# Attention scores from packed stationary tiles, with Q's products moved two sub-steps ahead

## The chip, the cores and the metric

The kernel runs on one core of a Trainium2 chip. The metric is the time of one execution on the device in microseconds (us). Three runs of the kernel before took 1155.66, 1157.41 and 1158.08 us, median 1157.41. The engines are TensorE (PE in the profile; its weight loads stand apart as PEld), VectorE (DVE), ScalarE (ACT), GpSimd (POOL) and SyncE (SP), which issues nearly all DMAs.

## The reference

Cross-attention of x (32 elements of 512 rows by 512) on a short context (32 by 77 by 512), 16 heads of depth 32, with a residual and a layer norm. In short:

```python
qh = _split_heads(q @ wq.T + bq, h)          # q: (32, 512, 512)
kh = _split_heads(k @ wk.T + bk, h)          # k = v = context: (32, 77, 512)
vh = _split_heads(v @ wv.T + bv, h)
scores = einsum('ntd,nsd->nts', qh, kh) / sqrt(32)
scores = scores + repeat(mask, h, axis=0)[:, None, :] * PAD
attn = softmax(scores, axis=-1)
ctx = einsum('nts,nsd->ntd', attn, vh)
out = _merge_heads(ctx, h) + q
out = (out - mean(out)) / sqrt(var(out) + 1e-5) * gamma + beta
```

## The kernel before

**Precision by parts.** Products are taken in fp32r, which keeps fewer bits than float32. So an operand is held as a high part (rounded) and a low part (what the rounding left), and a product is high times low plus low times high plus high times high: three matmuls (`terms`). This holds for Q, K, V and for the scores.

**Phase one** (0 to about 131 us) projects the context to K and V for all elements and stores both in scratch memory. K is masked, its mean over the kept keys is taken off (DVE sums, POOL makes `k_shift` from `shift_of_key` and adds it, ACT and DVE write the high and low parts). At its end two of the four column groups of the first element's Q are made.

**Phase two** runs a pipeline of steps over the elements; a loop does most of them, two a round. A step has 8 sub-steps, s = 0 to 7; h = s // 4 is one half of the heads (8 heads, two groups g of four), t = s % 4 is a tile of 128 rows of x. In each sub-step TensorE does, in this order:

- `q_half`: half of the product of one column group g of Q, 6 matmuls of 512 columns (two sub-steps make a group);
- `scores` of element a, half h, tile t: for each of two groups, three matmuls of 308 columns (four heads times 77 keys) with a 128-row piece of Q as weights; K stands as a block diagonal, `bd`, 32 rows of it to a head;
- `turn`: transposes of the exponents of the half before, a tile of up to 128 (head, key) pairs at a time, four transposes to a tile, five tiles to a half, by the table TURNS = ([], [0, 1], [2, 3], [4]) over t;
- `product`: attention times V for element a - 1, ten matmul instructions.

Beside it, ACT rounds Q from PSUM to `q_hi` with its bias (`high_q`), takes the exponent, copies turned tiles from `t_ps` to `pt` (`copy_pt`), rounds x (`high_x`) and normalises rows (`norm`). DVE makes `q_lo` (`q_low`), row maxima, the subtraction of the maximum, the scaling by the sum (`inv_sum`, `attn`), and the statistics. POOL makes the low part of x (`split_x`), adds x, and applies gamma and beta.

The order on each engine is that of its `step` function; nothing else schedules. PSUM has eight banks: two scores tiles of two banks each, two `t_ps`, one `q_ps`, one `o_ps`. A turn waits until the tile two before it has been copied out of its bank. The low and high parts of Q are for a group done in the sub-step after its second half, and the scores of the next half use them at once.

## Time and profile before

| | |
|---|---|
| median of three runs | 1157.41 us |
| the profiled execution | 1157.28 us, its span 1155.5 us |
| TensorE busy | 1123.1 us (97%) |
| weight loads | 1037.8 us (90%) |
| DVE, ACT, POOL busy | 822.1 (71%), 612.5 (53%), 771.8 us (67%) |
| mean granted TensorE clock | 0.988 of full |
| DMA | 141.07 MB, queue of SP 40.1% of 16 engines |

Busy time is what an engine's instructions cover. A matmul's time runs from its start to when its last result is written, and the next starts well before that; the pace of a stream of matmuls is therefore read from the starts of successive rows, or from the chain of waits, whose pieces follow one another without overlap.

### The profile page before, as it was taken

The page shows a single profiled execution, that of the slowest core. Times are in us where ns is not written, and L with a number is a line of the kernel's source. Part 1 is how long each engine was busy: PE and PEld are TensorE (multiplying, and loading weights), DVE is VectorE, ACT ScalarE, POOL GpSimd, SP SyncE. Part 2 cuts the span into 40 slices and gives each one's busy share as a digit, 9 for nine tenths or more (in the row PEclk, how much of TensorE's full clock was granted, in tenths as well). Part 3 has the DMA queues.
Part 4 walks back from the last instruction along what each step waited for, and adds up shares of the span by engine and source line. Part 5 has one row for each costly group of instructions (what it writes and reads, how often), then busy time and mean ns, then how long its engine had stood idle before and what let it go on. Part 6 is the DMA issues. An engine that isn't in the chain of part 4 may idle for free.

```text
span 1155.5 us, 25702 instructions
## 1 busy us (share of the span) xinstructions
PE 1123.1 (97%) x7541; PEld 1037.8 (90%) x7541; DVE 822.1 (71%) x1622; ACT 612.5 (53%) x1008; POOL 771.8 (67%) x667
## 2 busy tenths in 40 slices
PE   7899999999999999999999999999999999999994
PEld 7788789999999999999999999999999999999983
DVE  5776467777777777777777777777777777777786
ACT  3321254556566555555555656655555555565551
POOL 4999523677766676766667776667676666777465
PEclk9999999999999999999999999999999999999996
DMA  7745433233343444343344333344443334333223
GB/s 228 261 147 188 150 104 90 74 122 95 116 119 117 126 126 126 116 120 99 102 123 122 106 105 119 117 126 126 126 116 122 98 102 123 123 101 110 85 82 128
DMA packets 147207, 141.07 MB, mean 122 GB/s; under 512 B 86452, under 2 KB 88004, under 8 KB 147172
## 3 DMA queue, kind: packets, MB, share of 16 engines
q1 hardware_dynamic: 146564, 140.29, 40.1%
q10 hardware_dynamic: 608, 0.33, 0.1%
q8 instruction: 20, 0.33, 0.1%
q14 instruction: 15, 0.12, 0.0%
HBM read 91.71 MB, written 48.85 MB: 122 GB/s over the span
## 4 chain that ended last, share of the span: by engine, by line
PE 84%; DVE 2%; POOL 1%; issue 0%; ACT 0%; DMA 0%; DVEq 0%; SPq 0%; POOLq 0%
PE q_ps L724 31%; PE o_ps L765 23%; PE s_ps L740 18%; PE t_ps L751 12%; POOL x_lo L991 0%; DVE stats L822 0%; DVE attn L853 0%; PE q_ps L765 0%; DVE y L862 0%; DMA xT_raw<-in_xT 0%; DVE attn L814 0%; DVE row_max L885 0%; DVE y L868 0%; ACT q_hi L1030 0%; DVE y L843 0%
## 5 line engine op out<-in xcount | busy, mean ns | idle before, releaser
L765 PE MATMUL o_ps<-v_tiles,pt 128*128 128x66 f32 x2520 | 310.7, 270 | 1.5 <-DVE attn L814 1.5
L765 PEld LDWEIGHTS o_ps<-v_tiles,pt 128*128 128x128 f32 x2520 | 304.0, 192 | 1.9 <-issue 1.9
L885 DVE TENSOR_REDUCE row_max<-s_ps 128x8 f32<-128x616 f32 x256 | 203.2, 794 | 118.2 <-PE s_ps L740 118.1
L740 PE MATMUL s_ps<-bd,q_hi 128*128 128x308 f32 x1024 | 260.5, 305 | 1.1 <-ACT q_hi L1030 1.1
L991 POOL TENSOR_TENSOR x_lo<-xT_raw,x_hi 128x512 fp32r<-128x512 f32 x124 | 159.3, 1286 | 117.8 <-ACT x_hi L1026 117.7
L961 POOL TENSOR_TENSOR attn<-attn,x_rows 128x512 f32<-128x512 f32 x124 | 160.2, 1292 | 115.8 <-DVE attn L814 115.8
L1036 ACT COPY pt<-t_ps 128x512 f32<-128x512 f32 (+1 forms) x320 | 175.0, 588 | 107.1 <-PE t_ps L751 107.0
L1030 ACT ACTIVATE q_hi<-q_ps,bq_col 128x512 fp32r<-128x512 f32 x125 | 86.1, 689 | 254.9 <-PE q_ps L724 254.9
L724 PE MATMUL q_ps<-x_lo,wq_hi 128*128 128x512 f32 x500 | 218.7, 437 | 2.5 <-PEq L142 2.1
L1016 ACT ACTIVATE probs<-probs 128x616 f32<-128x616 f32 x256 | 183.3, 716 | 64.3 <-DVE probs L894 64.3
L894 DVE TENSOR_TENSOR probs<-s_ps,row_max 128x616 f32<-128x616 f32 x256 | 204.6, 799 | 5.7
L724 PE MATMUL q_ps<-x_hi,wq_lo 128*128 128x512 f32 x500 | 197.6, 395 | 0.0
L724 PE MATMUL q_ps<-x_hi,wq_hi 128*128 128x512 f32 x500 | 197.4, 395 | 0.0
L740 PEld LDWEIGHTS s_ps<-bd,q_hi 128*128 128x128 f32 x1024 | 181.1, 189 | 12.9 <-ACT q_hi L1030 1.5
L875 DVE SCALAR_TENSOR_TENSOR q_lo<-q_ps,bq_col,q_hi 128x512 fp32r<-128x512 f32 x125 | 93.8, 751 | 114.2 <-ACT q_hi L1030 114.2
L751 PE MATMUL t_ps<-ident,probs 128*128 128x128 f32 (+1 forms) x1280 | 171.9, 273 | 0.0
L969 POOL TENSOR_TENSOR y<-attn,gamma_all 128x512 f32<-128x512 f32 x123 | 158.5, 1288 | 13.8 <-ACT attn L1040 13.8
L972 POOL TENSOR_TENSOR y<-y,beta_all 128x512 f32<-128x512 f32 x123 | 158.5, 1289 | 9.6
L740 PE MATMUL s_ps<-bd,q_lo 128*128 128x308 f32 x512 | 156.3, 305 | 0.0
L751 PEld LDWEIGHTS t_ps<-ident,probs 128*128 128x128 f32 (+1 forms) x1280 | 151.1, 139 | 1.1
L814 DVE TENSOR_TENSOR attn<-o_ps,inv_sum 128x256 f32<-128x256 f32 x252 | 106.9, 424 | 17.9
L724 PEld LDWEIGHTS q_ps<-x_hi,wq_hi 128*128 128x128 f32 x500 | 94.1, 188 | 22.6
(96 smaller groups left out, 1292.9 us busy)
## 6 DMA issues: line engine op xcount, KB each, us to landing
xT_raw<-in_xT SPq DMA_DIRECT2D x128, 256.0 KB, 3.5
x_rows<-in_x SPq DMA_DIRECT2D x32, 1024.0 KB, 5.6
out<-y SPq DMA_DIRECT2D x128, 256.0 KB, 2.1
k_scratch<-k_out SPq DMA_DIRECT2D x8, 1232.0 KB, 5.4
bd<-k_scratch SPq DMA_DIRECT2D x128, 77.0 KB, 2.4
v_scratch<-v_out SPq DMA_DIRECT2D x16, 264.0 KB
v_tiles<-v_scratch SPq DMA_DIRECT2D x256, 9.9 KB
ctx_raw<-in_ctxT SPq DMA_DIRECT2D x3, 1232.0 KB, 6.2
```

What stands on the lines that cost most here:

```text
L724: mm = pe.matmul(q_bank(b, g)[:, :], (wq_hi, wq_lo)[u][:, k, P * g:P * g + P], x_part[v][:, k, :], start=(k == 0 and n == 0), stop=(k == K ...
L740: mm = pe.matmul(s_ps[t % 2][:, j, 0:GS], (q_hi, q_lo)[u][:, g, P * t:P * t + P], bd[par][:, v, g, :, :].rearrange("p h s -> p (h s)"), st ...
L751: mm = pe.transpose(t_ps[(NT * h + i) % 2][0:w, P * t:P * t + P], probs[h][:, t, P * i:P * i + w], ident[:, :])
L765: mm = pe.matmul(bank_of(b, t)[:, col:col + tile_cols[i]], pt[h][0:w, i, P * t:P * t + P], v_tiles[v_buffer(b, h)][0:w, i, 0:tile_cols[i]] ...
L885: dve.tensor_reduce(row_max[:, u, :].rearrange("p (j h) -> p j h", j=2), score_heads(t), AX.X, ALU.max).then_inc(max_ready, 1)
L894: dve.tensor_tensor(probs[h][:, t, :].rearrange("p (j h s) -> p j h s", j=2, s=S), score_heads(t), row_max[:, u, :].rearrange("p (j h) -> ...
L961: pool.tensor_tensor(attn[par][:, t, :], attn[par][:, t, :], x_rows[:, t, :], ALU.add).then_inc(resid_done, 1)
L969: pool.tensor_tensor(y[par][:, t, :], attn[par][:, t, :], gamma_all[:], ALU.mult).then_inc(scaled, 1)
L972: pool.tensor_tensor(y[par][:, t, :], y[par][:, t, :], beta_all[:], ALU.add).then_inc(out_ready, 1)
L991: pool.tensor_tensor(x_lo[par][:, k, :], xT_raw[:, k, :], x_hi[par][:, k, :], ALU.subtract).then_inc(x_lo_ready, 1)
L1016: act.activation(probs[h][:, t, :], probs[h][:, t, :], ACT.Exp).then_inc(exp_done, 1)
L1036: act.copy(pt[h][0:w, i, :], t_ps[(NT * h + i) % 2][0:w, :]).then_inc(pt_ready, 1)
```

## The change

**Packed weights for the scores.** The three products of a group of four heads used the array's 128 rows as four heads of 32 each. Now three tiles hold the parts of Q in another arrangement. `q_a`: rows 0 to 95 the high parts of heads 0 to 2, rows 96 to 127 a copy of head 0's high part. `q_c`: rows 0 to 95 the low parts of heads 0 to 2, rows 96 to 127 head 1's high part. `q_b`: head 3's high part, head 3's low part, head 2's high part, head 3's high part. K's tiles `k_ac` and `k_b` hold K's high or low parts to match. The matmuls with `q_a` and `q_c` write three heads (3 times 78 = 234 columns), the one with `q_b` writes heads 2 and 3 (156 columns). The 12 products of head parts are the same as before. A head takes 78 columns in place of 77 (`SW`).

**What it asks of the others.** A group's high part takes two ACT instructions (`q_a`, 96 partitions; `q_b`, 64), its low part two on DVE (96 and 32). Three DMAs for each pair of groups, issued by ACT (`move_q`), copy 32-row pieces within the on-chip memory; `scores` waits for them (`q_moved`). K of an element comes by 12 DMAs of 32 rows, before by 4 with twice the data each; they stand after x's in SP's order.

**Order of the work.** `q_of_step` puts Q's products two sub-steps earlier. Q has two PSUM banks (`q_ps`), turned tiles one (`t_ps`); a turn now waits for the copy of the tile just before it. The turns are spread as the tables TURNS_AHEAD and TURNS_BEHIND say (ahead of or behind the scores of the sub-step). `high_x` is at s = 2, 3, 4, 6, `norm` at s = 4, 6, 7 and at s = 0 of the next step; the store of row tile 1 and some of POOL's scaling move too. ACT does `copy_pt` before it issues `move_q`.

**Phase one.** POOL no longer makes `shift_of_key`: DVE multiplies each sum by the negative reciprocal count (`minus_mean_of_keys`). The zeroing of K's tiles comes after the first chunk, the mask's transposes after the first V tile. gamma and beta are loaded at the start of phase two, and DVE and POOL wait for them there (`scale_loaded`).

TensorE in the third sub-step (t = 2) of a step before: the rest of Q's half product, the scores of the element (`s_ps`), two turns (`t_ps`), the first products with V.

```order
L724 MATMUL q_ps<-x_hi,wq_hi 128x512
L740 MATMUL s_ps<-bd,q_hi 128x308 [waits k_loaded_0,shifted,q_lo_ready,q_hi_ready]
L740 MATMUL s_ps<-bd,q_lo 128x308
L740 MATMUL s_ps<-bd,q_hi 128x308 x2
L740 MATMUL s_ps<-bd,q_lo 128x308
L740 MATMUL s_ps<-bd,q_hi 128x308
L751 MATMUL t_ps<-ident,probs 128x128 [waits pt_ready,exp_done]
L751 MATMUL t_ps<-ident,probs 128x128 x3
L751 MATMUL t_ps<-ident,probs 128x128 [waits pt_ready,exp_done]
L751 MATMUL t_ps<-ident,probs 128x128 x3
L765 MATMUL o_ps<-v_tiles,pt 128x66 [waits attn_ready,v_loaded_0,pt_ready]
```

The same engine and sub-step now:

```order
L811 MATMUL q_ps<-x_hi,wq_hi 128x512
L842 MATMUL t_ps<-ident,probs 128x128 [waits pt_ready,exp_done]
L842 MATMUL t_ps<-ident,probs 128x128 x3
L828 MATMUL s_ps<-k_ac,q_a 128x234 [waits k_loaded_1,q_moved_0,shifted,q_lo_ready,q_hi_ready]
L828 MATMUL s_ps<-k_ac,q_c 128x234
L831 MATMUL s_ps<-k_b,q_b 128x156
L828 MATMUL s_ps<-k_ac,q_a 128x234
L828 MATMUL s_ps<-k_ac,q_c 128x234
L831 MATMUL s_ps<-k_b,q_b 128x156
L842 MATMUL t_ps<-ident,probs 128x128 [waits pt_ready,exp_done]
L842 MATMUL t_ps<-ident,probs 128x128 x3
L856 MATMUL o_ps<-v_tiles,pt 128x66 [waits attn_ready,v_loaded_0,pt_ready]
```

One turn has moved ahead of the scores; between the two turns, which share a bank, stand six narrower matmuls.

ACT in two sub-steps before, from the rounding of a group of Q on (`q_hi`; `pt` are copies of turned tiles, `probs` exponents):

```order
L1030 ACTIVATE q_hi<-q_ps,bq_col 128x512 [waits q_done]
L1016 ACTIVATE probs<-probs 128x616 [waits shifted]
L1036 COPY pt<-t_ps 128x512 [waits turned] x2
L1016 ACTIVATE probs<-probs 128x616 [waits shifted]
L1036 COPY pt<-t_ps 128x512 [waits turned] x2
```

ACT now, from the second sub-step to the third:

```order
L1136 ACTIVATE q_a<-q_ps,bq_col 96x512 [waits q_done]
L1138 ACTIVATE q_b<-q_ps,bq_col 64x512
L1153 COPY pt<-t_ps 128x512 [waits turned]
L1145 DMA q_a<-q_a 32x1024 [waits q_hi_ready]
L1146 DMA q_c<-q_a 32x1024
L1148 DMA q_b<-q_b 32x1024
L1116 ACTIVATE probs<-probs 128x616 [waits shifted]
L1153 COPY pt<-t_ps 128x512 [waits turned]
L1126 CAST x_hi<-xT_raw 128x512 [waits scores_done,xT_loaded_0]
L1153 COPY pt<-t_ps 128x512 [waits turned]
```

A group's rounding is two instructions, three DMA issues follow, and between the two copies of the third sub-step stands the rounding of x.

The diff, cut to its core:

```diff
-    GS = HG * S
+    GS = HG * (S + 1)
...
-    KDMA = HG * DMA
+    KDMA = 3 * HG * DMA
+    QDMA = 3 * DMA
...
-    KS = 6
+    KS = 5
+    SW = S + 1
+    QW = 3 * DH
...
+        q_a = sb(whole, "q_a", [P, NG, T], F32R)
+        q_b = sb(whole, "q_b", [P, NG, T], F32R)
+        q_c = sb(whole, "q_c", [P, NG, T], F32R)
+        k_ac0 = sb(whole, "k_ac0", [P, 2, NG, 3, SW], F32R)
+        k_b0 = sb(whole, "k_b0", [P, NG, 2, SW], F32R)
...
-                pool.tensor_tensor(shift_of_key[:], keep[:], neg_rcount[:].unsqueeze(3).broadcast_to([P, NG, 2, S]),
-                                   ALU.mult).then_inc(keep_set, 1)
-                pool.memset(bd0[:].bitcast(F32), 0.0).then_inc(bd_zeroed, 1)
...
-                        pool.tensor_tensor(k_shift[:], shift_of_key[:, m, :, :].unsqueeze(1).broadcast_to([P, HB // 2, 2, S]),
+                        pool.tensor_tensor(k_shift[:], keep[:, m, :, :].unsqueeze(1).broadcast_to([P, HB // 2, 2, S]),
...
+                    if c == 0:
+                        pool.memset(k_ac0[:].bitcast(F32), 0.0).then_inc(bd_zeroed, 1)
+                        pool.memset(k_b0[:].bitcast(F32), 0.0).then_inc(bd_zeroed, 1)
...
+                act.wait_ge(q_hi_ready, 4)
+                act.dma_start(q_a[QW:P, 0:2, :].bitcast(F32), q_a[0:DH, 0:2, :].bitcast(F32)).then_inc(q_moved[0], DMA)
+                act.dma_start(q_c[QW:P, 0:2, :].bitcast(F32), q_a[DH:2 * DH, 0:2, :].bitcast(F32)).then_inc(q_moved[0], DMA)
+                act.dma_start(q_b[0:DH, 0:2, :].bitcast(F32), q_b[QW:P, 0:2, :].bitcast(F32)).then_inc(q_moved[0], DMA)
...
+                    dve.wait_ge(k_totalled, n + 1)
+                    dve.tensor_tensor(k_sum[:, slot, :, :], k_sum[:, slot, :, :],
+                                      neg_rcount[:, n % NG, :].unsqueeze(1).broadcast_to([P, HB // 2, 2]), ALU.mult
                                       ).then_inc(k_summed, 1)
...
-            t_ps = [ps(two, f"t_ps{i}", [P, BANK]) for i in range(2)]
-            q_ps = ps(two, "q_ps", [P, BANK])
+            t_ps = ps(two, "t_ps", [P, BANK])
+            q_ps = [ps(two, f"q_ps{i}", [P, BANK]) for i in range(2)]
...
+            X_STEPS = (2, 3, 4, 6)
...
-            TURNS = ([], [0, 1], [2, 3], [4])
+            TURNS_AHEAD = ([], [], [2], [])
+            TURNS_BEHIND = ([0], [1], [3], [4])
...
             def q_bank(b, g):
-                return o_ps if isinstance(b, int) and b == 0 and g % 2 == 1 else q_ps
+                return q_ps[g % 2]
+            def q_of_step(s):
+                half, u = (s + 2) // 4, (s + 2) % 4
+                return (half + 1) // 2, (0 if half == 1 else 2) + u // 2, u % 2
...
+                    for ac in range(2):
+                        for h in range(3):
+                            rows = slice(DH * h, DH * h + DH)
+                            sp.dma_start(k_ac[par][rows, ac, :, h, 0:S].bitcast(F32), k_dram[b, rows, 0, :, :]
+                                         ).then_inc(k_loaded[par], DMA)
+                        rows = slice(DH * ac, DH * ac + DH)
+                        sp.dma_start(k_ac[par][QW:P, ac, :, ac, 0:S].bitcast(F32), k_dram[b, rows, 1, :, :]
                                      ).then_inc(k_loaded[par], DMA)
+                    for q in range(2):
+                        sp.dma_start(k_b[par][DH * q:DH * q + DH, :, 1, 0:S].bitcast(F32), k_dram[b, QW:P, 0, :, :]
+                                     ).then_inc(k_loaded[par], DMA)
+                        rows = slice(DH * (q + 2), DH * (q + 2) + DH)
+                        sp.dma_start(k_b[par][rows, :, q, 0:S].bitcast(F32), k_dram[b, rows, 1, :, :]
+                                     ).then_inc(k_loaded[par], DMA)
+                sp.dma_start(gamma_all[:], gamma.partition_broadcast(P)).then_inc(scale_loaded, DMA)
+                sp.dma_start(beta_all[:], beta.partition_broadcast(P)).then_inc(scale_loaded, DMA)
...
-                        used = b * 4 + g
-                        if isinstance(used, int) and used <= 4:
-                            used -= 1
-                        at_least(pe, q_hi_ready, used)
-                        at_least(pe, q_lo_ready, used)
+                        at_least(pe, q_hi_ready, b * 8 + (2 * g - 2))
+                        at_least(pe, q_lo_ready, b * 8 + (2 * g - 2))
...
-                    pe.wait_ge(q_hi_ready, b * 4 + (2 * h + 2))
-                    pe.wait_ge(q_lo_ready, b * 4 + (2 * h + 2))
+                    pe.wait_ge(q_hi_ready, b * 8 + (4 * h + 4))
+                    pe.wait_ge(q_lo_ready, b * 8 + (4 * h + 4))
+                    pe.wait_ge(q_moved[h], (b + 1) * QDMA)
                     pe.wait_ge(k_loaded[par], b * (KDMA // 2) + (KDMA - par * (KDMA // 2)))
                     at_least(pe, shifted, b * 8 + (4 * h + t - 1))
                     for j in range(2):
                         g = 2 * h + j
-                        for n, (u, v) in enumerate(terms):
-                            mm = pe.matmul(s_ps[t % 2][:, j, 0:GS], (q_hi, q_lo)[u][:, g, P * t:P * t + P],
-                                           bd[par][:, v, g, :, :].rearrange("p h s -> p (h s)"),
-                                           start=(n == 0), stop=(n == 2))
+                        for ac, q in ((0, q_a), (1, q_c)):
+                            pe.matmul(s_ps[t % 2][:, j, 0:3 * SW], q[:, g, P * t:P * t + P],
+                                      k_ac[par][:, ac, g, :, :].rearrange("p h s -> p (h s)"),
+                                      start=(ac == 0), stop=False, skip_group_check=True)
+                        mm = pe.matmul(s_ps[t % 2][:, j, 2 * SW:GS], q_b[:, g, P * t:P * t + P],
+                                       k_b[par][:, g, :, :].rearrange("p h s -> p (h s)"),
+                                       start=False, stop=True, skip_group_check=True)
                     mm.then_inc(scores_done, 1)
                 def turn(b, h, i):
                     pe.wait_ge(exp_done, b * 8 + (4 * h + 4))
-                    at_least(pe, pt_ready, b * (2 * NT) + (NT * h + i - 1))
+                    at_least(pe, pt_ready, b * (2 * NT) + (NT * h + i))
...
                         h, t = s // 4, s % 4
-                        qb = a + h
-                        g = (2 if h == 0 else 0) + t // 2
-                        if real(qb) and not in_phase_one(qb, g):
-                            q_half(qb, g, t % 2, (par + h) % 2)
+                        ahead, g, part = q_of_step(s)
+                        if real(a + ahead) and not in_phase_one(a + ahead, g):
+                            q_half(a + ahead, g, part, (par + ahead) % 2)
...
+                        if real(a - 1 + h):
+                            for i in TURNS_AHEAD[t]:
+                                turn(a - 1 + h, 1 - h, i)
                         if real(a):
                             scores(a, h, t, par)
...
                         if real(a - 1 + h):
-                            for i in TURNS[t]:
+                            for i in TURNS_BEHIND[t]:
                                 turn(a - 1 + h, 1 - h, i)
...
-                    dve.wait_ge(q_hi_ready, b * 4 + (g + 1))
-                    dve.scalar_tensor_tensor(out=q_lo[:, g, :], in0=q_bank(b, g)[:, :], scalar=bq_col[:, g:g + 1],
-                                             in1=q_hi[:, g, :], op0=ALU.add, op1=ALU.subtract
+                    dve.wait_ge(q_hi_ready, b * 8 + (2 * g + 2))
+                    dve.scalar_tensor_tensor(out=q_c[0:QW, g, :], in0=q_bank(b, g)[0:QW, :], scalar=bq_col[0:QW, g:g + 1],
+                                             in1=q_a[0:QW, g, :], op0=ALU.add, op1=ALU.subtract
                                              ).then_inc(q_lo_ready, 1)
+                    dve.scalar_tensor_tensor(out=q_b[DH:2 * DH, g, :], in0=q_bank(b, g)[QW:P, :],
+                                             scalar=bq_col[QW:P, g:g + 1], in1=q_b[QW:P, g, :],
+                                             op0=ALU.add, op1=ALU.subtract).then_inc(q_lo_ready, 1)
...
+                dve.wait_ge(scale_loaded, 2 * DMA)
...
+                pool.wait_ge(scale_loaded, 2 * DMA)
...
+                    if g == 0:
+                        at_least(act, scores_done, b * 8 - 4)
+                    if g == 2:
+                        at_least(act, scores_done, b * 8)
+                    act.activation(q_a[0:QW, g, :], q_bank(b, g)[0:QW, :], ACT.Identity, bias=bq_col[0:QW, g:g + 1]
                                    ).then_inc(q_hi_ready, 1)
+                    act.activation(q_b[P // 2:P, g, :], q_bank(b, g)[P // 2:P, :], ACT.Identity,
+                                   bias=bq_col[P // 2:P, g:g + 1]).then_inc(q_hi_ready, 1)
+                def move_q(b, h):
+                    act.wait_ge(q_hi_ready, b * 8 + (4 * h + 4))
+                    g = slice(2 * h, 2 * h + 2)
+                    act.dma_start(q_a[QW:P, g, :].bitcast(F32), q_a[0:DH, g, :].bitcast(F32)).then_inc(q_moved[h], DMA)
+                    act.dma_start(q_c[QW:P, g, :].bitcast(F32), q_a[DH:2 * DH, g, :].bitcast(F32)
+                                  ).then_inc(q_moved[h], DMA)
+                    act.dma_start(q_b[0:DH, g, :].bitcast(F32), q_b[QW:P, g, :].bitcast(F32)).then_inc(q_moved[h], DMA)
...
                         if real(a - 1 + h):
-                            for i in TURNS[t]:
+                            for i in TURNS_AHEAD[t]:
                                 copy_pt(a - 1 + h, 1 - h, i)
+                        for k in range(KC):
+                            if X_STEPS[k] == s and real(a + 2):
+                                high_x(a + 2, k, par)
+                        ahead, g, part = q_of_step(s)
+                        high = part == 1 and real(a + ahead) and not in_phase_one(a + ahead, g)
+                        if high:
+                            high_q(a + ahead, g)
+                        if real(a - 1 + h):
+                            for i in TURNS_BEHIND[t]:
+                                copy_pt(a - 1 + h, 1 - h, i)
+                        if high and g % 2 == 1:
+                            move_q(a + ahead, g // 2)
```

## Rows read from the trace of the kernel before

**Rows 1.** The page, part 1: busy us (share of span) xinstructions.

```profile
PE 1123.1 (97%) x7541; PEld 1037.8 (90%) x7541; DVE 822.1 (71%) x1622; ACT 612.5 (53%) x1008; POOL 771.8 (67%) x667
```

**Rows 2.** The chain of waits that ended last, 690 to 725 us: start, us, what.

```profile
691.72 1.45 PE q_ps L724 x6
693.17 0.85 PE s_ps L740 x6
...
694.89 1.06 PE o_ps L765 x10
...
722.98 1.45 PE q_ps L724 x6
```

**Rows 3.** Timeline, TensorE, 693 to 696 us: start, us, engine, line, op, tiles, count.

```profile
693.15 0.30 PE L740 MATMUL s_ps<-bd,q_lo 128*128 128x308 f32 x1
...
693.85 1.04 PE L751 MATMUL t_ps<-ident,probs 128*128 128x128 f32 x8
694.73 1.23 PE L765 MATMUL o_ps<-v_tiles,pt 128*128 128x66 f32 x10
```

**Rows 4.** The same stretch, weight loads.

```profile
693.15 0.33 PEld L740 LDWEIGHTS s_ps<-bd,q_hi 128*128 128x128 f32 x2
...
694.62 1.20 PEld L765 LDWEIGHTS o_ps<-v_tiles,pt 128*128 128x128 f32 x10
```

**Rows 5.** Groups by line and shape: busy us, mean ns | idle before.

```profile
L740 PE MATMUL s_ps<-bd,q_hi 128*128 128x308 f32 x1024 | 260.5, 305 | 1.1 <-ACT q_hi L1030 1.1
...
L765 PE MATMUL o_ps<-v_tiles,pt 128*128 128x99 f32 x1008 | 209.3, 289 | 0.0
...
L1036 ACT COPY pt<-t_ps 128x512 f32<-128x512 f32 x256 | 137.5, 589 | 104.5 <-PE t_ps L751 104.5
...
L875 DVE SCALAR_TENSOR_TENSOR q_lo<-q_ps,bq_col,q_hi 128x512 fp32r<-128x512 f32 x125 | 93.8, 751 | 114.2 <-ACT q_hi L1030 114.2
...
L1030 ACT ACTIVATE q_hi<-q_ps,bq_col 128x512 fp32r<-128x512 f32 x125 | 86.1, 689 | 254.9 <-PE q_ps L724 254.9
...
L1036 ACT COPY pt<-t_ps 104x512 f32<-104x512 f32 x64 | 37.5, 585 | 2.6 <-PE t_ps L751 2.5
```

**Rows 6.** Stretch of two elements: us, then busy us of PE, PEld, DVE, ACT, POOL.

```profile
691.50:754.10 62.60, 62.60 (x435) 58.23 (x434) 45.31 (x93) 36.45 (x60) 42.93 (x37) 1.00 0.38 116
```

**Rows 7.** Timeline, 713 to 715 us, a turn and its copies.

```profile
713.72 1.04 PE L751 MATMUL t_ps<-ident,probs 128*128 128x128 f32 x8
...
714.35 1.07 ACT L1036 COPY pt<-t_ps 128x512 f32<-128x512 f32 x2 [1.34 <-PE t_ps L751]
```

**Rows 8.** Timeline, 1111 to 1113 us, a wait of TensorE.

```profile
1111.65 0.42 DVE L814 TENSOR_TENSOR attn<-o_ps,inv_sum 128x256 f32<-128x256 f32 x1
...
1112.22 1.30 PE L765 MATMUL o_ps<-v_tiles,pt 128*128 128x66 f32 x10 [0.50 <-DVE attn L814]
```

**Rows 9.** Timeline, 37 us, a wait of TensorE in phase one.

```profile
37.51 0.48 PE L522 MATMUL v_ps<-wv_lo,ctx_hi 128*104 128x512 f32 x1 [2.98 <-DVE v_out L420]
```

**Rows 10.** Stretch behind it: us, busy us by engine; after them the granted clock.

```profile
37.50:41.00 3.50, 3.49 (x10) 2.46 (x11) 2.04 (x4) 1.26 (x3) 3.06 (x5) 0.61 0.92 310
```

**Rows 11.** Timeline: DMA issues by ACT (4 us), phase two's start.

```profile
3.99 0.89 ACTq L339 DMA_DIRECT2D keep<-in_mask  x2
...
132.33 0.47 PE L724 MATMUL q_ps<-x_lo,wq_hi 128*128 128x512 f32 x1 [2.09 <-PEq L142]
...
135.67 5.04 POOL L991 TENSOR_TENSOR x_lo<-xT_raw,x_hi 128x512 fp32r<-128x512 f32 x4
```

**Rows 12.** Timeline of SP's DMA issues, 690 and 720 us.

```profile
690.47 2.89 SPq L670 DMA_DIRECT2D bd<-k_scratch  x4
...
720.65 0.38 SPq L661 DMA_DIRECT2D out<-y  x1
```

**Rows 13.** DMA issues: count, KB each, median us to landing.

```profile
bd<-k_scratch SPq DMA_DIRECT2D x128, 77.0 KB, 2.4
...
gamma_all<-in_gamma SPq DMA_DIRECT2D x1, 256.0 KB, 5.4
```

More of the change, by code:

```diff
@@ L96, in xattn @@
         q_lo_ready = sem("q_lo_ready")
+        q_moved = [sem(f"q_moved_{i}") for i in range(2)]
         x_hi_ready = sem("x_hi_ready")
@@ L688, in step @@
                                      ).then_inc(x_loaded, DMA)
+                    if real(a + 1) and not in_phase_one(a + 1):
+                        load_keys(a + 1, 1 - par)
                     if real(a - 3):
+                        store(a - 3, 1, 1 - par)
                         store(a - 3, 2, 1 - par)
@@ L1035, in copy_pt @@
                     w = tile_rows[i]
-                    act.copy(pt[h][0:w, i, :], t_ps[(NT * h + i) % 2][0:w, :]).then_inc(pt_ready, 1)
+                    act.copy(pt[h][0:w, i, :], t_ps[0:w, :]).then_inc(pt_ready, 1)
                 def norm(b, t, par):
```

197 lines of the change are left out of this document (119 added, 78 removed).

## The prediction

> **What bounds the kernel now.** I read the page first: TensorE is busy 97% of the span, its weight loads 90%, no other engine over 71% [rows 1]. Then the chain of waits inside the loop: in 690 to 725 us it holds TensorE pieces alone, six matmuls for Q (1.45 us), six for the scores (0.85), ten for V (1.06), with turns between, and the same place of the next element comes 722.98 - 691.72 = 31.26 us later [rows 2]. Two elements take 62.60 us and TensorE is busy in all of them, at full clock (1.00); DVE is busy for 45.31 of them, ACT for 36.45, POOL for 42.93 [rows 6]. So in the loop every nanosecond that TensorE's stream loses or gains is the kernel's, until another engine comes late.
>
> Last, the paces. A score matmul of 308 columns takes 0.85 / 6 = 0.141 us [rows 2]. Its row says 305 ns, since a row runs to the last result, about 0.16 us past the next one's start. A transpose of 128 columns takes (694.73 - 693.85) / 8 = 0.109 us [rows 3]. V's weight loads: 1.20 us for ten, one alone 0.33 - 0.14 = 0.19, so (1.20 - 0.19) / 9 = 0.112 us each [rows 4]. These matmuls have 66 and 99 columns, the transposes 128, and all come at 0.11: it is the weight load that paces them, and the columns do not show.
>
> **Term A, the narrower scores.** Still three matmuls for a group, 1536 in all in 512 groups, but of 234, 234 and 156 columns in place of 308 each. None of them should be paced by its columns: 308 cost 0.141, 512 cost 1.45 / 6 = 0.242, that is 0.0005 us a column, which puts 234 at 0.104 and 156 at 0.066. Both lie below the load's 0.112. So a group costs 3 x 0.112 = 0.336 in place of 0.423, and 512 groups save 512 x 0.087 = **44.5 us**. Bounds: if the load did not pace them, 0.274 a group and -76 us; above, no gain at all (0.141 stays the price), or a loss (the third rival). The trace has no fp32r matmul under 308 columns. I take the load's pace, since it holds for 66, 99 and 128 columns.
>
> The row pair at 693.15 shows a weight load starting with the matmul before it, which is still running, at the same rows of the array [rows 3, 4]. The Trainium skill, TensorE: Matmul & The Clock Gate, section "Packing small matmuls — row/col tiling", says that a load overlaps matmuls in flight only when it goes to another row group. By that a group would cost its loads and its columns one after the other, about 0.34 + 0.27 = 0.61, and the change would lose 96 us; but 308 columns and a load at 0.141 together already contradict it.
>
> The same page, section "Back-to-back issue gap", gives a sustained 81 ns a matmul at 128 columns and 131 at 512. By it (an estimate) a group costs 0.27, and A is -78 us. The rows disagree at both ends: 109 ns at 128 columns, 242 at 512 [rows 2, 3].
>
> **Term B, a new wait between two turns.** With one `t_ps` bank a turn waits for the copy of the one before. Four of the five have a product or Q's matmuls between them. Turns 2 and 3 have only the scores. From turn 2's start: its four transposes take 4 x 0.109 = 0.44, the last result is there at 0.61 (the eight of [rows 7] last 1.04 = 8 x 0.109 + 0.17), the copy starts 0.03 later (714.35 against 714.32 by the same sum) and takes 0.589 [rows 5, 7], so it ends at 1.23. From a release to TensorE's next matmul it takes 1112.22 - 1112.07 = 0.15, and a stream that restarts is 0.07 longer (1.30 against 1.23 for the same ten) [rows 3, 8]: 1.45. Without the wait turn 3 would start at 0.44 + 6 x 0.112 = 1.11. The loss is 0.34, two times an element: 64 x 0.34 = **+21.8 us**. It is not less if ACT is busy when the tile comes, only more. At that point ACT has behind it the exponent and the three DMA issues, about 0.47 each (0.89 for two [rows 11]); they end about 1.2 us into the sub-step and turn 2 ends at 1.45 + 0.61. So ACT is free, with some 0.2 us to spare behind the exponent. Behind the waiting turn on TensorE stand its product and the next Q half; all slip with it. Bounds: 0 (if I am wrong on the copy) and 0.6 each, 38 us.
>
> **Term C, more work for DVE and ACT.** A group's low part is now two instructions; partitions do not shorten one (ACT's copy takes 589 ns on 128 and 585 on 104 partitions [rows 5]). DVE: 8 more in two elements at 751 ns, less 0.08 of overlap, 5.4 us: 45.31 + 5.4 = 50.7 of about 61 us, 83% [rows 5, 6]. ACT: 8 more roundings at 689 ns less 0.10 of overlap, 4.7, and 12 DMA issues at 0.47, 5.6: 46.7 of 61. Both hold on average. They are close in the odd sub-steps, the more so as DVE's statistics fall in two of them (s = 1, 7); the product then waits for `attn`, since `o_ps` is one bank. I take **+1.5 us**, bounds 0 and +25. The Q parts themselves have two sub-steps, about 7.5 us, where they had none. The on-chip copies of 128 KB each should land in 2.4 us, as K's 77 KB did [rows 13], or in twice that, and are covered. Gone with `q_ps` as a single bank is a wait that the loop did not have: nothing.
>
> **SP.** K's load goes from 4 issues in 2.89 us [rows 12] to 12 of half the size, some 6 us. The queue is 9 us idle between V's pieces and the store at 720.65 [rows 12]. What it is moved past, x's loads and the residual's, starts 2.9 us sooner; K has until the next step. Nothing.
>
> **Term D, phase one.** TensorE waits 2.98 us for `v_out` at 37 us [rows 9], and the 3.50 us behind it ran at clock 0.61 [rows 10], which is 1.4 us lost at 1.2 GHz. The wait ends a chain that starts with POOL's `shift_of_key` and the zeroing, both gone from there. I take **-4 us**, bounds 0 and -4.4.
>
> **Term E, the start of phase two.** ACT and DVE each have two instructions more, and ACT three DMA issues, between the last Q product and the barrier: +1.2. Then DVE and POOL wait for gamma and beta, 5.4 us from issue to landing [rows 13], the second 0.4 later; POOL's four `x_lo` take 5.04 [rows 11]. They would end about 10.7 us after the barrier. TensorE now wants them after four Q halves and two scores, 4 x 1.45 + 2 x 0.67 = 7.1. That is a wait of about 3.5, where 1.06 stood (for Q's high part [rows 5]). With another half-clock stretch of 1.5 possible I take **+4.5 us**, bounds 0 and +8.
>
> **The sum**, against the profiled execution's own 1157.3 us (the median is 1157.4, so it stands for the runs): 1157.3 - 44.5 + 21.8 + 1.5 - 4 + 4.5 = **1136.6 us**. An element takes 31.26 - 1.39 + 0.68 + 0.05 = 30.6 us.
>
> **Rivals.**
> 1. The turn's wait does not show (the copies come in time): for it, before a turn had 0.87 us of other work around it and no wait; against it, the sum of B, made of rows. Time 1136.6 - 21.8 = 1114.8. Chance 0.17.
> 2. DVE is the bound where both statistics and low parts fall. For it: in sub-step 7 its instructions sum to about 4.1 us against 3.6 of TensorE's. Against it: sub-steps 2 to 4 give it back. If each element loses 0.6 us more, 32 x 0.6 = 19 us: 1155.8. Chance 0.11.
> 3. The other side: a narrow fp32r matmul runs at the price of a plain float32 one. The place is the scores of every sub-step. The nearest row is V's 99 columns, float32, 289 - 162 = 127 ns, 1.28 ns a column [rows 5]. A group of 624 columns is then 0.80, +0.377 x 512 = +193, and the turn's wait is covered: 1157.3 + 193 + 1.5 + 0.5 = 1352 us. It decides from the point at which a group costs over 0.423 less the rest of the sum, about 0.38. Against it: the cost of 308 and of 512 columns falls with the columns. For it: only that no row lies under 308. Chance 0.12.
> 4. The change doesn't do what it says: narrow matmuls keep 0.141. Then A is 0, and with 0.85 between the turns B is 64 x 0.16 = 10.4: 1157.3 + 10.4 + 1.5 - 4 + 4.5 = 1169.7. Chance 0.05.
>
> **How the numbers follow.** My forecast has 0.55; by its own bounds it lies between 1122 and 1150. The predicted time is 1136.6. The range runs from 1108, below rival 1 by the bounds of D and E, to 1158, which takes in rival 2; it leaves out rivals 3 and 4. A difference of 0.2% (2.3 us) is about what a measurement of this kernel can tell from none. Faster: 0.55 + 0.17 + 0.07 of rival 2 = 0.79; same: the rest of rival 2, 0.04; slower: rivals 3 and 4, 0.17.
>
> **What would show it.** A: six score matmuls in about 0.67 us between the first score and what follows. B: waits of TensorE for ACT's `pt`, 64 of them, some 0.34 us each, in the third sub-step of each half, and none at the other turns. C: DVE near 83% with no wait of TensorE for it. D: no wait for `v_out` at 37 us and no half clock behind it. E: one wait for `x_lo` of some 3 us early in phase two. I am wrong if the six take more than 0.8 us, if DVE's `attn` or ACT's exponent shows up as what TensorE waits for in the loop, or if the turns wait over 0.6 us.

## The result and the profile after

The changed kernel takes 1148.68 us (median of six runs, 1145.06 to 1151.02), the kernel before, run beside it, 1155.0: a ratio of 0.994, 95% interval 0.992 to 0.996. Measured again later it was 1147.84 against 1155.88, ratio 0.9925 (0.990 to 0.995). So it is 6 to 8 us faster, where 21 were forecast. The profiled execution took 1145.06, span 1143.3.

The page after, part 1, answers to [rows 1] (busy us, share of the span, instructions), and part 4, the chain that ended last, by engine:

```profile
PE 1095.9 (96%) x7541; PEld 989.2 (87%) x7541; DVE 941.6 (82%) x1782; ACT 726.6 (64%) x1136; POOL 770.0 (67%) x668
...
PE 56%; DVE 14%; issue 8%; ACT 7%; ACTq 3%; DVEq 0%
```

TensorE is still busy nearly all the time, but it holds only 56% of the chain. The chain after, 690 to 725 us, a part of what stood as TensorE alone in [rows 2] (start, us, what):

```profile
698.94 1.45 PE q_ps L811 x6
700.39 0.22 PE s_ps L828 x2
...
712.81 0.80 DVE row_max L981
...
714.36 0.74 DVE q_c L968
715.13 0.76 DVE q_b L971
715.92 0.22 DVE inv_sum L895
...
719.70 0.67 ACT q_a L1136
...
721.10 0.53 ACT pt L1153
721.65 0.61 ACTq L1146
722.29 0.63 ACTq L1148
...
723.67 0.56 ACT pt L1153
724.28 0.66 PE t_ps L842 x4
```

The pieces between TensorE's work are DVE's low parts, ACT's rounding of Q and its DMA issues. That is the list of suspects, not yet the causes. The waits of TensorE in 500 to 900 us, 13 elements (engine and line, what it waited for, us in total, times, longest):

```profile
PEld t_ps L842 <- ACT pt L1153: 6.0, 26, 0.4
PEld t_ps L842 <- issue: 3.2, 13, 0.3
PEld o_ps L856 <- issue: 1.3, 6, 0.2
PEld o_ps L856 <- DVE attn L907: 1.1, 7, 0.2
PE t_ps L842 <- ACT pt L1153: 0.7, 3, 0.3
```

There are three kinds, at four places of an element: turn 3 behind the copy of turn 2 (twice), turn 0 of sub-step 0 behind the exponent (once; the view says "issue" there, but the matmul starts 0.13 us after ACT's exponent ends, in nearly every element), and the product of sub-step 4 behind `attn` (once).

One number carries all that follows: the time of one element in the loop, taken from the start of the 25th score cluster (a sub-step's six matmuls) to that of the 249th, 28 elements. Before: (1096.42 - 220.21) / 28 = 31.29 us. After: (1083.91 - 224.26) / 28 = 30.70. The forecast was 0.66 less an element; it is 0.59 less. The loop nearly kept its promise, but by errors that cancelled, as the runs show. What else is missing lies at the start of phase two and at the end.

### The profile page after: what moved, and what is told of

Read it like the earlier page. It is cut to its first block, busy times and chain, and to the rows that moved or that the text cites. A ratio compares the mean times of both kernels' runs of the same rounds, so it can differ in the third digit from the quotient of the medians.

```text
span 1143.3 us, 26963 instructions
## 1 busy us (share of the span) xinstructions
PE 1095.9 (96%) x7541; PEld 989.2 (87%) x7541; DVE 941.6 (82%) x1782; ACT 726.6 (64%) x1136; POOL 770.0 (67%) x668
## 3 DMA queue, kind: packets, MB, share of 16 engines
q1 hardware_dynamic: 167044, 145.36, 44.5%
## 4 chain that ended last, share of the span: by engine, by line
PE 56%; DVE 14%; issue 8%; ACT 7%; ACTq 3%; DVEq 0%
PE q_ps L811 21%; PE o_ps L856 16%; PE t_ps L842 9%; PE s_ps L828 7%; DVE row_max L981 4%; ACT pt L1153 3%; DVE probs L990 2%; PE s_ps L831 2%; DVE stats L915 2%; DVE q_b L971 2%; ACT q_a L1136 2%; ACTq L1148 2%; ACTq L1146 2%; DVE q_c L968 1%; ACT q_b L1138 1%
## 5 line engine op out<-in xcount | busy, mean ns | idle before, releaser
L856 PE MATMUL o_ps<-v_tiles,pt 128*128 128x66 f32 x2520 | 314.0, 272 | 1.0 <-DVE attn L907 0.8
L1153 ACT COPY pt<-t_ps 128x512 f32<-128x512 f32 (+1 forms) x320 | 186.9, 584 | 82.1 <-PE t_ps L842 76.6
L842 PE MATMUL t_ps<-ident,probs 128*128 128x128 f32 (+1 forms) x1280 | 200.4, 280 | 12.4 <-ACT pt L1153 5.0
L842 PEld LDWEIGHTS t_ps<-ident,probs 128*128 128x128 f32 (+1 forms) x1280 | 140.0, 140 | 35.5 <-ACT pt L1153 11.7
L828 PE MATMUL s_ps<-k_ac,q_a 128*128 128x234 f32 x512 | 155.2, 303 | 3.5 <-DVE q_c L968 3.5
L828 PE MATMUL s_ps<-k_ac,q_c 128*128 128x234 f32 x512 | 141.3, 276 | 0.0
L1136 ACT ACTIVATE q_a<-q_ps,bq_col 96x512 fp32r<-96x512 f32 x126 | 85.6, 680 | 81.7 <-PE s_ps L831 59.7
L831 PE MATMUL s_ps<-k_b,q_b 128*128 128x156 f32 x512 | 123.0, 240 | 0.0
L811 PEld LDWEIGHTS q_ps<-x_lo,wq_hi 128*128 128x128 f32 x504 | 96.2, 191 | 16.7 <-issue 5.1
```

The costliest lines, as they stand in the source:

```text
L811: mm = pe.matmul(q_bank(b, g)[:, :], (wq_hi, wq_lo)[u][:, k, P * g:P * g + P], x_part[v][:, k, :], start=(k == 0 and n == 0), stop=(k == K ...
L828: pe.matmul(s_ps[t % 2][:, j, 0:3 * SW], q[:, g, P * t:P * t + P], k_ac[par][:, ac, g, :, :].rearrange("p h s -> p (h s)"), start=(ac == 0 ...
L842: mm = pe.transpose(t_ps[0:w, P * t:P * t + P], probs[h][:, t, P * i:P * i + w], ident[:, :])
L856: mm = pe.matmul(bank_of(b, t)[:, col:col + tile_cols[i]], pt[h][0:w, i, P * t:P * t + P], v_tiles[v_buffer(b, h)][0:w, i, 0:tile_cols[i]] ...
L1153: act.copy(pt[h][0:w, i, :], t_ps[0:w, :]).then_inc(pt_ready, 1)
```

## Experiments

"After" is 1148 us in the differences below, "an element" the number just defined; every ratio is to the kernel before, with its 95% interval.

| run | median us | ratio | an element |
|---|---|---|---|
| narrow matmuls alone, in the kernel before | 1106.63 | 0.957 (0.955-0.959) | 29.67 |
| moves issued by SyncE | 1141.67 | 0.988 (0.986-0.990) | 30.65 |
| turn 3 behind the product | 1149.02 | 0.994 (0.993-0.996) | 30.79 |
| low parts later | 1138.78 | 0.986 (0.984-0.988) | 30.48 |
| after, again | 1147.84 | 0.9925 (0.990-0.995) | 30.69 |
| low parts later and turn 3 behind | 1120.62 | 0.970 (0.968-0.972) | 29.87 |
| that and scaling early | 1116.39 | 0.966 (0.964-0.968) | 29.67 |
| that and moves by SyncE | 1117.37 | 0.967 (0.965-0.968) | 29.67 |
| one low part | 1138.46 | 0.986 (0.984-0.988) | 30.43 |
| one rounding | 1141.65 | 0.989 (0.987-0.991) | 30.62 |
| one of each | 1128.42 | 0.977 (0.975-0.979) | 30.12 |

### Narrow matmuls alone

```diff
-  s_ps[..., 0:GS], q[...], bd[...]                    # 308 columns, three times
+  first, end = (0, 234) if n < 2 else (GS - 156, GS)  # 234, 234, 156
+  s_ps[..., first:end], q[...], bd[...][:, first:end]
```

> The kernel before with nothing changed but the columns of its three score matmuls: 0 to 234, 0 to 234 and 152 to 308 in place of 308 each. What is left out: two of the three products for a part of the columns, so the scores are not the reference's. It prices term A with no other part of the change. Theory (from the trace after, where six score matmuls take 0.63 us when nothing waits, against 0.85 before): 0.22 us less in 256 sub-steps, -56 us, ratio 0.951, with no wait of TensorE in the loop, since ACT and DVE have their old work. Rival 1 (the price in my prediction, every one at the weight load's 0.112): -44.5 us, 0.961. Rival 2 (the shorter stream runs into another engine here already): less than 35 us, with waits of TensorE in the loop.

Measured: -50.0 us. The chain, 690 to 700 us:

```profile
690.70 1.45 PE q_ps L724 x6
692.16 0.63 PE s_ps L741 x6
692.78 1.10 PE o_ps L766 x10
693.89 1.44 PE q_ps L724 x6
695.33 0.63 PE s_ps L741 x6
695.96 0.89 PE t_ps L752 x8
```

Six matmuls take 0.63 us where they took 0.85 [rows 2], no wait of TensorE stands in the loop, and the product and the turns behind take 0.02 to 0.04 more than before. An element takes 1.62 us less. This is term A; it was worth 50 in the median (52 by the element), not 44.5, and not the 56 of the bare 0.22 either.

Where the difference comes from is seen in single rows. The matmuls of one cluster in the kernel after, where nothing waits, and the weight loads of one in this run:

```profile
136.90 0.27 PE L828 MATMUL s_ps<-k_ac,q_a 128*128 128x234 f32 x1
137.00 0.28 PE L828 MATMUL s_ps<-k_ac,q_c 128*128 128x234 f32 x1
137.12 0.24 PE L831 MATMUL s_ps<-k_b,q_b 128*128 128x156 f32 x1
137.19 0.31 PE L828 MATMUL s_ps<-k_ac,q_a 128*128 128x234 f32 x1
137.34 0.27 PE L828 MATMUL s_ps<-k_ac,q_c 128*128 128x234 f32 x1
```

```profile
692.10 0.30 PEld L741 LDWEIGHTS s_ps<-bd,q_hi 128*128 128x128 f32 x2
692.33 0.19 PEld L741 LDWEIGHTS s_ps<-bd,q_lo 128*128 128x128 f32 x1
692.44 0.19 PEld L741 LDWEIGHTS s_ps<-bd,q_hi 128*128 128x128 f32 x1
692.55 0.75 PEld L766 LDWEIGHTS o_ps<-v_tiles,pt 128*128 128x128 f32 x6
```

Inside the cluster the loads come every 0.11 us, as the prediction took it. The matmul behind the one of 156 columns starts 0.07 to 0.08 us after it, but the next one then 0.15, so inside a cluster nothing is won by that: over the loop the first five gaps add up to 0.56 us, five times 0.112. Only the last gap, to the product or the turn, is 0.078 where the forecast had 0.112. That is 0.034 a cluster, less what the matmuls behind give back.

In the Trainium skill, TensorE: Matmul & The Clock Gate, section "Packing small matmuls — row/col tiling", one sentence says that loads overlap matmuls in flight only in another row group. This trace contradicts it: six loads and matmuls at the same rows took 0.63 us together. (The same section elsewhere lets a load for the array's background weight buffer go ahead; no run here tells which buffer a load went to.)

### Moves issued by SyncE, and turn 3 behind the product

```diff
 # ACT's step
-  if high and g % 2 == 1: move_q(a + ahead, g // 2)
 # SyncE's step, ahead of load_keys and ahead of the first store
+  move_q(a, 1) ... move_q(a + 1, 0)
```

> The kernel after with the three on-chip copies of Q's parts issued by SyncE (ahead of K's load and ahead of the first store) in place of ACT, in the loop; those of phase one stay on ACT. It takes 1.85 us of issue off ACT two times an element. Theory (what TensorE waits for at the end of these chains is one t_ps bank, ACT's crowded seventh sub-step and DVE's low parts, and the issues lie in a sub-step where ACT has room): the exponent behind them comes up to 0.6 us earlier, but the copy of turn 2 behind it only some 0.05, so -2 to -5 us of the time after, ratio to before 0.990 to 0.993. Rival (the chain of waits taken at its word, where ACT's DMA issues and the idle behind them hold some 5% of the span): -17 us or more, ratio 0.98.

-6 us in the median, but only 0.05 an element, which is 1.6. The two profiled executions differ by 1.4 us, so the traces do not show where the rest of the median is; it stays open, as far as it is not the scatter of the end (below). The chain's share for ACT's DMA issues was no measure of what they cost: the copy of turn 2 that stands behind them in sub-step 2 starts about 0.08 us after its tile is ready (0.28 in three elements of 28), and 0.04 with the moves on SyncE.

```diff
-TURNS_BEHIND = ([0], [1], [3], [4])
+TURNS_BEHIND = ([0], [1], [], [4])
+TURNS_LAST = ([], [], [3], [])      # behind product(a - 1, h, t)
```

> The kernel after with the fourth of five turns moved behind the product of its sub-step, on TensorE, and its copy ahead of the next exponent on ACT. Between the two turns that share a sub-step stands then the scores and a product. It prices term B. Theory: the wait of 0.24 us net and the slower restart of 0.055 behind it go, two times an element, 0.57 us x 32 = -18 us of the time after, ratio to before 0.979. Rival 1 (the wait only moves, to the turn that now has Q's half alone between it and the next, or to the exponent behind the moved copy on ACT): 0 to -6 us. Rival 2: ACT's copy, now ahead of the exponent, delays turn 0 of the next half: slower than after.

Nothing is gained and 0.09 an element lost: rival 1, in a form I had not named. The two places went different ways: sub-step 6 takes 0.19 less (3.75 us for 3.94), sub-step 2 takes 0.28 more (4.27 for 3.98). The timeline in sub-step 2, with turn 3 gone from between scores and product:

```profile
724.23 0.76 DVE L975 SCALAR_TENSOR_TENSOR q_b<-q_ps,bq_col,q_b 32x512 fp32r<-32x512 f32 x1
...
725.62 0.42 DVE L911 TENSOR_TENSOR attn<-o_ps,inv_sum 128x256 f32<-128x256 f32 x1
...
726.19 0.55 PE L857 MATMUL o_ps<-v_tiles,pt 128*128 128x66 f32 x3 [0.41 <-DVE attn L911]
```

The product, now due earlier, waits for `attn`, which stands on DVE behind the two low parts of the sub-step before. Turn 3's wait had covered that one.

### Low parts later, then with the turn, then with the scaling

```diff
 # DVE's step: q_low from the end of odd sub-steps to behind the next scale_attn
+  low = {2: (a, 3), 4: (a + 1, 0), 6: (a + 1, 1), 0: (a, 2)}.get(s)
+  if low ...: q_low(*low)
```

> The kernel after with DVE's two instructions for Q's low part moved from the end of their sub-step to behind the next one's inv_sum and attn. Nothing is added or taken away. It tests whether the second low-part instruction costs the product that waits for o_ps (sub-step 4: 0.23 us an element in the trace after). Theory: that wait goes, 0.23 x 32 = -7.4 us of the time after, ratio to before 0.987, and no other place gets worse by over 0.1 us an element. Rival (DVE is full over the stretch, so the order doesn't matter): 0, the wait comes back as a later row_max and a later exponent.

-9 us, an element 0.22 less: the wait of sub-step 4 is gone from the trace, as forecast.

> The kernel after, unchanged, on the chip of the next three runs: their base, and a second trace of it. Theory: the loop's element takes 30.67 us again and every sub-step the same to 0.02, and what differs between two executions lies before 165 us and behind 1090 us, where TensorE's clock steps. Rival: the loop itself varies by more than 0.1 us an element.

The second trace agrees with the first: 30.69, and on average no sub-step of the loop differs by over 0.02 us.

> The kernel after with two edits that were tried singly: Q's low part behind the next inv_sum and attn on DVE, and the fourth turn behind the product on TensorE (its copy on ACT now behind the next exponent). Theory (the first edit frees o_ps in time, which is what took back the second one's gain when it was alone): both waits go, 0.57 + 0.23 = 0.80 us an element, -25 us of the time after, ratio to before about 0.972. Rival (DVE is full around the statistics, so the product goes on waiting for attn): what the low parts alone gave, ratio 0.986.

-27 us, 0.83 an element. One edit alone gained 0.22, the other alone lost 0.09. Sub-step 2, where the moved turn alone had uncovered the wait for `attn`, now takes 3.65. One thing besides the pairing differs: ACT copies turn 3 behind the next exponent here and ahead of it in the run of the turn alone. That copy falls into sub-steps 3 and 7, which differ by 0.04 us at most between the two runs, so it hardly carries the result; no run separates it. The waits in 500 to 900 us shrink to one line, turn 0's:

```profile
PEld t_ps L843 <- issue: 2.6, 13, 0.2
```

```diff
 # ACT's step, s == 7
+  norm(a - 2, 2, par)      # now ahead of high_q, was behind copy_pt
   high_q(a + ahead, g)
```

> The run before it with one more edit: ACT's scaling of an attention row in the eighth sub-step stands ahead of Q's rounding, where ACT was idle for about 1 us, and no more between the copy and the next exponent. Theory: the exponent that turn 0 waits for comes 0.8 us earlier, and turn 0's wait of 0.32 us an element goes: -10 us of that kernel's time, -35 of the time after, ratio to before 0.963. Rival (the scaling waits for POOL's shift there and now holds Q's rounding, or DVE's probs comes last anyway): 0 to -3 us of that kernel's time.

0.20 an element, 4.2 us in the median (less than the 10 I gave it, since turn 0's wait and its restart had 0.25 in this kernel). TensorE has no wait left in the loop, and an element takes 29.67 us, exactly what it took with the narrow matmuls alone in the kernel before. So in this order the added instructions, the DMA issues, the single `t_ps` bank and K's smaller loads cost the loop nothing; all of the 1.03 us an element that the change lost against the narrow matmuls is taken back by order alone. The page's parts 1 and 4:

```profile
PE 1073.7 (97%) x7541; PEld 985.9 (89%) x7541; DVE 940.6 (85%) x1782; ACT 711.5 (64%) x1136; POOL 768.7 (69%) x668
...
PE 82%; DVE 2%; issue 1%; ACT 1%; DMA 1%; POOL 0%; SPq 0%; ACTq 0%; DVEq 0%; POOLq 0%
```

This kernel beats both: 0.966 of before, 0.973 of after, by order alone. Run again later it was 0.968 (0.966 to 0.970). DVE is busier (85%) than where it was the trouble (82%).

> The run before it with the copies of Q's parts issued by SyncE in the loop. Theory: in the loop they gate nothing now, 0 to -2 us; the start and the end gain what they gained when it was the only edit (1 to 5 us): -1 to -7 us of that kernel's time. Rival: with the other waits gone the issues on ACT are what is left, over -8 us.

0.00 an element and +1 us: the issues on ACT gate nothing.

### What the added instructions cost

```diff
-  q_c low ... .then_inc(q_lo_ready, 1); q_b low
+  q_c low ... .then_inc(q_lo_ready, 2)            # one low part
-  q_a high ... .then_inc(q_hi_ready, 1); q_b high
+  q_a high ... .then_inc(q_hi_ready, 2)           # one rounding
```

> The kernel after without DVE's second low-part instruction for every element but the first (left out: the low part of the fourth head's Q, which stays the first element's). It prices the added instruction by itself. Theory: the product's wait for attn in sub-step 4 (0.23 us an element) goes as it did when the instructions were only put later: -6 to -9 us of the time after, and DVE is busy for 91 us less. Rival 1: DVE's work as such costs (0.76 us x 4 an element): over -20 us. Rival 2: only the order mattered and one instruction is still in the way: 0.

> The kernel after without ACT's second rounding for every element but the first (left out: the fourth head's high part). Theory: the exponent that turn 0 waits for in sub-step 0 comes 0.7 us earlier and turn 0's 0.32 us go: -8 to -10 us of the time after; turn 3's wait stays. Rival: the exponent waits for DVE's probs anyway (DVE's low parts start earlier here, which helps): over -15 us or near 0.

> Both left out. ACT and DVE then have the counts of instructions for Q that they had before. It prices all of term C in the loop but for the DMA issues. Theory: the two waits are at two different places (sub-steps 4 and 0) and add up: -16 to -19 us of the time after; what is left to the kernel before with narrow scores alone is the one t_ps bank, 0.5 us an element. Rival: they overlap, -10 us.

In these three runs the fourth head's low part, its high part, or both are left out for every element but the first. One low part less: 0.27 an element, as expected. One rounding less: 0.08, a miss. Turn 0's wait in sub-step 0 went, but the product of the same sub-step now waits for `attn`: the sub-step takes 3.84 us, after 3.90, and 3.60 with both left out (waits, 500 to 900 us):

```profile
PEld t_ps L845 <- ACT pt L1157: 5.1, 26, 0.2
PEld o_ps L859 <- issue: 4.2, 20, 0.2
PEld o_ps L859 <- DVE attn L910: 1.2, 7, 0.2
```

Both: 0.58, far over the 0.35 of the parts, and only turn 3's wait is left:

```profile
PEld t_ps L845 <- ACT pt L1158: 5.3, 27, 0.2
```

So the added rounding and low part cost 0.58 an element, 18.7 us over 32, and the one `t_ps` bank 30.12 - 29.67 = 0.45, 14.4 us. This split of the 1.03 depends on the order of taking away, since the waits cover each other: with the low parts later, moving the turn was worth 30.48 - 29.87 = 0.61.

### The start of phase two

From the last matmul of phase one to the ninth score cluster it is 27.8 us before, 36.15 and 36.17 in the two traces after, 35.9 and 36.1 in those of the fastest kernel (scaling early). The chain after:

```profile
137.20 0.75 DVE q_c L968
137.98 0.76 DVE q_b L971
138.76 0.81 DVE row_max L981
139.60 0.81 DVE probs L990
140.43 0.72 ACT probs L1116
141.18 0.68 ACT q_a L1136
141.89 0.69 ACT q_b L1138
142.60 0.75 DVE q_c L968
143.38 0.76 DVE q_b L971
144.17 0.81 DVE row_max L981
```

Here DVE and ACT work in turn, each waiting for the other, with three groups' parts in series up to 149.3 us. The fifth cluster, at 149.41, also needs the moves: the last was issued at 143.81 and landed 5.4 us later, that is over the twice 2.4 us within which the prediction called them covered. The next runs change the fastest kernel for the first element alone (its second group pair); the first leaves the moves out, the second the added rounding and low part, the third both.

> The fastest kernel so far (low parts later, fourth turn behind the product, scaling early) without the copies of the second half of Q's parts of the first element alone; those partitions hold zeros for that element, so its scores for four heads are not the reference's. It prices the wait for these copies in the fifth sub-step of phase two, and what TensorE's clock does behind it. Theory: the fifth score cluster starts about 3 us earlier against the fourth, and the half-clock stretch behind it goes too: -4 us, 0.4% of that kernel's time. Rival 1: the next late thing there (x_lo, the exponent) takes its place: 0 to -1. Rival 2: the clock falls all the same: -3.

> The fastest kernel without ACT's second rounding and DVE's second low part for the second half of Q's groups of the first element alone (two groups; those rows hold zeros there, so four heads' scores of that element are not the reference's). It prices the chain at the start of phase two, which in the trace after runs from 135.7 to 149.4 us through ACT and DVE in turn, with three groups' parts in it. Theory: the chain loses 2 x (0.69 + 0.76) = 2.9 us, and the sixth score cluster comes 2.5 to 3 us earlier after the start of phase two: -2.5 to -4 us. Rival (the moves of Q's parts, which the fifth cluster waits for, hold it): the fifth cluster stays, less than -1.

> The same, and without the first element's copies of Q's second half either (which alone brought the fifth cluster 2.9 us forward and left the sixth where it was). Theory: nothing more than the run before at the sixth cluster, -2.5 to -4 us in all, since the chain of ACT and DVE sets it. Rival: the two costs were each other's cover, as in the loop, and together give -6 us.

To the ninth cluster: 35.3, 34.9 and 33.3 us, so -0.7, -1.1 and -2.7 against about 36.0. Measured from the fourth cluster, the fifth came 2.5 to 2.9 earlier without the moves, and the sixth 0.2 at most. Both of my theories for the single edits missed. Together they gave more than their sum, so each cost was in part the other's cover, as the rival of the third says, but far short of its 6 us. The medians (1114.9, 1114.0, 1115.6, ratios 0.965, 0.967, 0.966; the fastest kernel 1116.4 and 1118.6, ratios 0.966 and 0.968) can't tell these sizes, and the reason stands in the last 60 us. Two executions of the fastest kernel (window, us, busy us of PE, PEld, DVE, ACT, POOL, then the granted clock):

```profile
1055.00:1111.00 56.00, 36.53 (x260) 34.74 (x259) 43.38 (x89) 21.02 (x34) 33.16 (x28) 0.76 0.36 120
```

```profile
1055.00:1117.00 62.00, 42.35 (x270) 40.28 (x268) 44.62 (x91) 21.41 (x34) 34.26 (x29) 0.70 0.33 109
```

From the 249th cluster to the end it took 58.3 and 63.0 us, while up to that cluster the two agree to 1.0 us. The same holds over all 17 traces: in the ten whose mean granted clock from there on is 0.75 or more that stretch took 58.2 to 59.4 us, in the five with 0.72 or less 61.4 to 63.2, in the two between 59.6 and 59.8. That the clock is the cause, and not a companion of other waits, is not shown.

## Why the prediction was wrong

**Term A, -44.5: right in kind, 5 to 7 us short.** The load's pace of 0.112 held inside the cluster; what it did not hold for is the last gap, 0.078. In the trace after, the six take 0.63 to 0.64.

**Term B, +21.8: measured 14.4** with Q's extra instructions left out, and 19.5 (0.61 an element) by the other way of taking it away; at the places named and nowhere else. The step that was too large is the release: I took 0.15 us from the end of a copy to the next matmul, from another wait, and here turn 3 starts 0.05 after the copy of turn 2 ends (724.28 against 723.67 + 0.56). Turn 3 starts 1.28 us behind turn 2; 1.23 + 0.15 would be 1.38. A tenth of a microsecond at 64 places is 6 us. And "it is not less if ACT is busy, only more" was false as a price: with the product's wait for `attn` behind it, taking this wait away gained nothing.

**Term C, +1.5: this is the step that failed.** It measured 18.7, inside its bounds of 0 to 25 but twelve times its value. The busy sum under it was right for DVE: 50.7 of about 61 us forecast, 51.8 of 61.4 measured, and partitions do not shorten its instruction (0.737 us on 96 partitions, 0.756 on 32, 0.751 on 128):

```profile
691.50:752.90 61.40, 60.95 (x434) 55.16 (x433) 51.76 (x101) 43.67 (x68) 42.88 (x37) 1.00 0.56 149
```

The step from 83% to "+1.5" was not right. TensorE waits for single answers (DVE's `attn` frees `o_ps`, ACT's exponent feeds turn 0), and an instruction added in front of such an answer cost time here although DVE was idle for a sixth of the loop, and ACT for more. The prediction saw "close in the odd sub-steps", wrote a like mechanism down as rival 2 at 0.6 an element, chance 0.11, and gave it 0.05 in the sum. It measured 0.58. Of this, sub-step 0 had 0.30 (the exponent, and `attn` close behind it), sub-step 4 had 0.22 (`attn`) and sub-step 2 the rest, the first two behind Q's parts, not in sub-step 7 among the statistics where rival 2 put it. DVE was not the bound either: with the same instructions in another order the loss is zero at 85%. "I am wrong if DVE's `attn` or ACT's exponent shows up" was met.

In the loop A + B + C came to 0.59 an element against 0.66, since +17 in C met -7 in B and -7 in A (1.62 x 32 = 52). That the loop's sum came out near the forecast was luck.

**Term D, -4: right.** The wait for `v_out` and the half clock behind it are gone, and a new wait of 1.5 us for `keep_v` stands at 32.8 us; the second stretch of K matmuls starts 3.44 us earlier (38.50 against 41.94).

**Term E, +4.5: 8.4 in the two traces,** and for other reasons. The barrier came 2.2 later against the last matmul, not 1.2. The wait for `x_lo` was 0.4, not 3.5: TensorE itself needed 9.0 us to get there, part of it at half clock. In its place came the series of Q's parts and the moves; what they cost in the second half of the first element is 2.7 (measured in the fastest kernel). And two more halves of Q, 2.9 us, now stand ahead of the first scores; the prediction costed "two sub-steps ahead" at nothing. The second half-clock stretch, which the prediction held possible, came too: 149 to 153 us ran at a mean granted clock of 0.57, before at 1.00. Its price is not separated: the second trace after was at half clock for longer there (0.57 over 149 to 157 us) and reached the ninth cluster in the same time.

The two Q halves are taken out near the end, but nothing comes back there: from the 249th cluster on the traces after take 59.4 and 58.2, before 59.0, though the score clusters are 0.2 us shorter each and two Q halves are gone. The chain there holds more of DVE's work on the last rows than of TensorE's. The narrow matmuls alone, with the old order of Q, end in 58.3, so the moved halves show neither way at the end; no run tested them by themselves.

**The sum.** The two profiled executions differ by 12.2: -3.45 (D), +8.4 (E), -17.4 (30 elements of the loop), +0.3 (end). The forecast had -4, +4.5 and -21.2, 20.7 in all. Of the 8.5 missing, 3.9 are E, 3.8 the loop. The other 4 to 6 us up to the medians are scatter of single executions: 1141.2 to 1151.0 for the kernel after in twelve runs, the fastest at a mean granted clock of 0.989, the slowest at 0.977, and the profiled ones were among the fastest. That this scatter lies at the end is read from the 17 traces; ten of these twelve executions have none. The prediction took one execution as standing for the median; of before it was 2.3 us above it, of after 3.6 below. So the number was missed at the start of phase two (E), in the loop and by this; the mechanism was missed in C, and errors the other way in A and B hid that.

Rivals: 1 (no wait at the turn) did not occur; 3 and 4 are excluded by 0.63 us. (In rival 4, 64 x 0.16 is 10.2, not 10.4.)

## What to carry to other kernels

The same added instructions on DVE and ACT cost 19 us or nothing by their order alone, with DVE at 82% or 85%. For each added instruction ask which answer to the bound engine now stands behind it, and walk the one sub-step where that is due, in times, before trusting an average. Two waits near each other cover one another, so an edit that removes one may show nothing (here even +0.09 us an element) and two together 27 us: test them in pairs before dropping either. A chain of waits names suspects, not prices: ACT's DMA issues held 3% of it and were worth 0.05 us an element.

## What was not expected of the hardware

- Down to 156 columns fp32r matmuls stay at the pace of their weight loads, 0.11 us each. A matmul behind one of 156 columns starts 0.076 us after it and the next one 0.148, so the gap of a single pair misleads; two gaps together are again 0.224.
- From the end of a copy on ACT to the matmul that waited for it took 0.05 us, where 0.15 was read behind `attn` on DVE [rows 8] and 0.13 behind ACT's exponent.
- DMA issues on ACT took 0.51 to 0.61 us each in the loop (medians by line, single ones to 0.84), where two in phase one took 0.89 together [rows 11]. They cost the loop 0.05 us an element.
- Behind the same work, the stretch from the 249th cluster to the end of one kernel took 58.3 or 63.0 us; the windows above have a mean granted clock of 0.76 and 0.70.
